# Attention on one core: the high part of the probabilities is weighed by all 128 columns of the values in one product

## The reference, cut to what matters

```python
q, k, v = tok(q), tok(k), tok(v)          # 16384 pixels x 48 channels
q = _l2norm(q)
k = _l2norm(k)
attn = jnp.einsum('bnc,bmc->bnm', q, k) * temperature
attn = jax.nn.softmax(attn, axis=-1)
out = jnp.einsum('bnm,bmc->bnc', attn, v)
```

## Time and profile before

| what | value |
|---|---|
| median of three runs | 7481.2 us |
| the profiled execution's own time | 7482.72 us |
| its span, from the first to the last instruction | 7480.9 us |
| TensorE matmul busy | 6171.0 us, 82% |
| TensorE weight load busy | 2683.0 us, 36% |
| VectorE busy | 6842.5 us, 91% |
| ScalarE busy | 5235.5 us, 70% |
| GpSimd busy | 3435.1 us, 46% |
| mean granted TensorE clock | 0.948 of 2.4 GHz |

### The profile page before, as it was taken

How to read it: one execution, slowest core, us unless ns; L and a number is a source line. 1 busy time by engine, 2 the same in 40 slices (tenths; PEclk the granted TensorE clock), 3 DMA queues, 4 the chain that set the end, 5 groups by cost and what they waited for, 6 DMA issues and landing times. The chain is left out here.

```text
span 7480.9 us, 170231 instructions
## 1 busy us (share of the span) xinstructions
PE 6171.0 (82%) x69312; PEld 2683.0 (36%) x69312; DVE 6842.5 (91%) x6229; ACT 5235.5 (70%) x5309; POOL 3435.1 (46%) x1811
## 2 busy tenths in 40 slices
PE   6899999999999999799668888888888888866330
PEld 3333333333333333366323333333333333333220
DVE  7799999999999999899779999999999999986776
ACT  3388888888888888633468888888888888842000
POOL 2000000000000000100169999999999999974777
PEclk9899999999999999899889999999999999987665
DMA  2200000000000000000110000000000000022333
GB/s 42 61 8 8 8 11 8 8 8 8 8 11 8 8 8 8 4 0 0 45 49 6 6 6 6 6 6 6 6 6 6 6 6 6 6 57 74 83 84 81
DMA packets 129089, 146.51 MB, mean 20 GB/s; under 512 B 52077, under 2 KB 111245, under 8 KB 127261
## 3 DMA queue, kind: packets, MB, share of 16 engines
q1 hardware_dynamic: 102848, 82.30, 4.1%
q0 software_dynamic: 24576, 50.36, 2.6%
q10 hardware_dynamic: 960, 3.74, 0.3%
HBM read 98.55 MB, written 37.75 MB: 18 GB/s over the span
## 5 line engine op out<-in xcount | busy, mean ns | idle before, releaser
L1753 POOL TENSOR_TENSOR k_image<-k_image,s_b 128x1024 f32<-128x1024 f32 x1152 | 2700.6, 2355 | 117.9 <-ACT k_image L1666 83.3
L705 ACT ACTIVATE att_prob<-att_scores,a_bound,a_temp 128x1024 f32<-128x1024 f32 x2048 | 2354.8, 1201 | 421.9 <-PE att_scores L648 421.9
L716 DVE TENSOR_TENSOR att_prob_lo<-att_prob 128x1024 f16<-128x1024 f32 x2048 | 2431.9, 1237 | 157.3 <-ACT att_prob L705 141.7
L633 POOL TENSOR_TENSOR k_image<-k_image,att_rden 48x512 f32 x32 | 67.7, 2115 | 2987.5 <-DVE att_rden L728 2987.5
L1666 ACT COPY k_image<-h_du 128x1024 f32<-128x1024 f32 x1152 | 1166.2, 1012 | 322.5 <-PE h_du L1600 321.9
L1716 DVE TENSOR_TENSOR_SCAN h_state_odd<-h_keep,k_image 128x1024 f32<-128x1024 f32 x576 | 1366.2, 2470 | 0.0
L648 PE MATMUL att_scores<-att_queries,att_keys 32*128 32x512 f16 (+1 forms) x20480 | 1294.2, 378 | 21.4 <-DMA att_queries<-qk_halves 18.8
L1672 ACT ACTIVATE h_keep<-h_keep,h_decay 128x1024 f32<-128x1024 f32 x1152 | 1256.7, 1091 | 74.7 <-PE h_keep L1589 51.0
L665 PE MATMUL att_sums<-att_prob,a_values 128*64 128x512 bf16 x8192 | 1125.4, 395 | 0.0
L1589 PE MATMUL h_keep<-h_rows,h_spread 128*128 128x512 bf16 x2304 | 698.8, 385 | 511.8 <-DVE h_state_odd L1716 263.2
L1600 PE MATMUL h_du<-h_rows,h_spread 128*128 128x512 bf16 x2304 | 701.2, 386 | 37.0 <-DMA h_rows<-parts 34.8
(11 more groups left out here) (296 smaller groups left out, 7026.6 us busy)
## 6 DMA issues: line engine op xcount, KB each, us to landing
y_rows<-h_y_sb SPq DMA_DIRECT2D x1024, 3.0 KB
att_queries<-qk_halves SPq DMA_DIRECT2D x124, 128.0 KB, 2.2
parts<-t_part SPq DMA_DIRECT2D x48, 192.0 KB, 2.5
h_rows<-parts SPq DMA_DIRECT2D x128, 72.0 KB
b_shared<-cells,b_index POOLq DMA_INDIRECT x512, 2.6
qk_halves<-qkv_hi SPq DMA_DIRECT2D x128, 48.0 KB, 1.6
cells<-b_shared SPq DMA_DIRECT2D x4, 1536.0 KB, 5.1
att_keys<-qk_halves SPq DMA_DIRECT2D x32, 128.0 KB, 3.0
```

The lines of the kernel that those rows point to most:

```text
L705: nc.scalar.activation(prob[:, u % RING, :], scores[:, u % SLOTS_S, :], ACT.Exp, bias=bound[:, 0:1], scale=temp[:, 0:1]).then_inc(prob_rea ...
L716: nc.vector.tensor_tensor(prob_lo[:, u % RING, :], prob[:, u % RING, :], prob_hi[:, u % RING, :], ALU.subtract).then_inc(low_ready, 1)
L1753: nc.gpsimd.tensor_tensor(drive[k % 3], du_sb[k % 3], b[:, c * CH:(c + 1) * CH], ALU.mult).then_inc(drive_ready, 1)
```

## The change

For each of the two key tiles of a unit, the two products of the high probabilities with the two sides of the values become one product with all 128 columns, into all 128 partitions of `sums`. The operands, the order of the products, the accumulation and the semaphores stay. The low product and the scores are as before.

```diff
                 for r in range(2):
-                    for side in range(2):
-                        part = slice(side * CHUNK, (side + 1) * CHUNK)
-                        nc.tensor.matmul(sums[part, slot, :], values[:, key_tile(u, r), part],
-                                         prob_hi[:, u % RING, r * BLK:(r + 1) * BLK], start=g == 0 and r == 0, stop=False)
+                    nc.tensor.matmul(sums[:, slot, :], values[:, key_tile(u, r), :],
+                                     prob_hi[:, u % RING, r * BLK:(r + 1) * BLK], start=g == 0 and r == 0, stop=False)
```

## The result

The changed kernel takes 7554.14 us (median, 7548.36 to 7556.47) against 7481.24 before: +72.9 us, a ratio of 1.0095 with a 95% interval of 1.0083 to 1.0107. The forecast was 7530, slower, with 7488 to 7575 as the range. The sign, the place and the mechanism were right; the size came out at about one and a half times the 49 us that I had summed.

What follows compares the result with a forecast made beforehand. TensorE's walk from wave to wave was taken as the bound, VectorE in part. 1024 pairs x 0.075 = 76.8 us, less 27.6 for the vanished stall, gave +49 us: 7530, with 7488 to 7575 for eight in ten.

Steps and rivals of the forecast that it cites:

- What bounds the kernel: Attention's inner part: TensorE's walk, 2.655 us a pair, bounds about 30 pairs of 32; VectorE stalls it 0.89 a block.
- Streaming and loads: High product: four waves remain, halved records save nothing; loads lie under earlier products except at layout changes, gaining hundredths there.
- Scores to high: Step from the last score wave to the first high wave, rows to full array: kept at 0.31 us.
- High to low: Step from the last high to the first low wave, full array to 64-column tiles: 0.31 us, today 0.22.
- x: Added time per pair of units on TensorE: 0.075 us, low end 0.055, high end 0.115.
- low to low: Step between the two low waves, then the first behind a layout change: 0.24 us, today 0.22.
- three steps within the high product: Steps between the four full-array high waves: 0.68 us together, between 0.66 and 0.72 (today's).
- The refund: Slower TensorE no longer stalls for VectorE: 0.89 us a block given back in 31 blocks, 27.6 us.
- The low product's waits for VectorE: Sign in the profile after: these waits should fall from 75.6 us to a few.
- The faster one: Rival: full array to column tiles costs nothing, high to low stays 0.22; -18 us, 7463; chance 0.10.
- The case of no difference: Rival: load half exposed, high to low about 0.27, small first step; within 15 us, 7466 to 7496; chance 0.09.
- The heavier case: Rival: high product's steps or rows-to-full-array change cost more; over 0.12 us a pair, more than 7575; chance 0.04.

Runs made afterwards that it cites:

- the third experiment: Kernel before the change, with a block's reciprocals and divisions spread over 40 units in place of 32: 7457.15 us against 7489.74, ratio 0.9959.
- the fourth experiment: Changed kernel with its reciprocals and divisions spread over 40 units in place of 32: 7559.8 us against 7489.74 for the kernel before, ratio 1.0095.
- the second experiment: Changed kernel with the low products of a pair placed ahead of the high ones: 7558.41 us, ratio 1.0091 to the kernel before.
- the fifth experiment: Against the kernel with half the key tiles in full-array form: products reordered, five layout changes a pair in place of three; 7789.95 us, ratio 1.0399 to the kernel before.

## Why the prediction was right, and where it was off

**What bounds the kernel.** Right. TensorE's walk from wave to wave sets the attention, though no view of idle or busy time says so. It was seen in the starts: the steady pairs take the same time, and the steps add up to it without a remainder.

**Streaming and loads.** Right. Half the records brought nothing, because the two sides ran in one wave, and of 150 us less of weight loading nearly all lay under the products. The exception is the first step behind the change from the scores. There the load isn't hidden, and it takes 96 ns in place of 108; the step fell from 0.251 to 0.238, so 0.013 us a pair, about what the prediction allowed for.

**Scores to high.** I bounded a change that the trace didn't hold, from rows to the full array, by the changes that it did hold, 0.31. It is 0.32 by rows in hundredths, and by the medians no dearer than today's change from rows to column tiles (0.318 against 0.317). Every change of layout behind 512 columns of f16 or bf16 in these kernels lies between 0.31 and 0.35.

**High to low.** Here the cost was placed, and it was there: 0.32 for 0.22. The low product's next step was expected to grow to 0.24, and did.

**The size.** The term that was mis-sized is x, the lengthening of a pair, and in it the saving within the high product. By the blocks x is 2.753 - 2.653 = 0.100 us in place of 0.075. Medians over the steady pairs of both traces give it step by step:

| step | forecast | measured |
|---|---|---|
| high to low | 0.22 to 0.31, +0.09 | 0.228 to 0.316, +0.088 |
| low to low | 0.22 to 0.24, +0.02 | 0.215 to 0.240, +0.025 |
| three steps within the high product | 0.72 to 0.68, -0.04 | 0.704 to 0.690, -0.014 |

No other step moved by more than 0.002. The three add up to 0.07 forecast (0.075 as I had it, since the new walk of 2.73, in rounded steps, was set against a period of 2.655 and not against the old walk's 2.66) and 0.099 measured. So the two dear steps were right, and nearly all that was missing is the saving of 0.04, of which 0.014 came. I had leaned toward line 1600, whose moving operand lies contiguous (0.23); with the strided high half the first step is 0.238 and the others 0.226. The 0.72 of today was itself too much by rounding: its rows in hundredths give steps of 0.26, 0.22 and 0.24, the medians 0.251, 0.226 and 0.227. 1024 pairs make 26 us of the 0.025 between 0.075 and 0.100, less 2 by which the refund was larger: the miss of 24.

**The refund.** Right, and shown from both sides by the spreading: 27.6 us forecast; 31 x 0.96 = 30 us by the blocks and 33 by the run times (the third experiment), and nothing left to gain after the change (the fourth).

**What I said to look for.** The block is 89.15 us where I had 88.4, the same miss times 32. One sign misled. The low product's waits for VectorE should have fallen from 75.6 us to a few. The group of its loads after the change names VectorE for 233.0 us. But each of these waits is the 0.44 us between the last load of the high product and the low one's, which the change of layout makes; the products themselves show no idle time on line 670, and a block has no remainder. In the fourth experiment, with a block of the same length, the same idle time of these loads (455 us with "issue") is put down to VectorE for 136.7 us only, so the name carries nothing. It is the false name that the exp of line 705 bore before, and I should have expected it here.

**The rivals.** The faster one, a free change from the full array to column tiles, is refuted by the step of 0.32 and by the second experiment. The case of no difference needed a step from high to low of about 0.27; it is 0.32. The heavier case, over 0.12 a pair, came about, among the kernels with three changes of layout, only with 120 columns, through the slower load.

## What to carry to other kernels

Two column-tiled products that share a wave already use the whole array; to merge them into one saves no time in streaming, and where the neighbours on TensorE are tiled, it adds a change of layout, here 0.10 us each time. Count changes of layout as well as waves, keep products of one layout together, and read both from the starts of the waves. Before a slower engine is blamed or a faster one praised, look for a stall between it and its partner: here one hid 30 us of the loss, and moving a few small operations of VectorE gained 33 us where the edit to TensorE lost 73.

## What the runs showed that I had not expected

Eight columns fewer made the kernel 34 us slower: a load of 120 columns takes 131 ns, one of 128 takes 96. Where weights are padded with zeros anyway, 128 columns are the better width, wherever a load can't be hidden.

A change of layout costs 0.09 to 0.10 us at the step itself, whatever the load behind it takes (96, 108 or 131 ns) and whichever the direction: outside the fifth experiment, where both parts fall into one step, the medians of these steps are 0.312 to 0.319 us, against 0.215 within one layout, or 0.226 behind the strided operand. The step behind it adds 0.01 to 0.05, and that part grows with the load: 0.012 with 96 ns, 0.025 with 108, 0.048 with 131. What happens in the 0.09, a drain as the Trainium skill (TensorEngine Tiling (Array Packing), Key Properties) has it or something else, no run here tells.
